# Second attention: values stationary in four 32-column array tiles, sums by a constant pattern, inverses spread by block transposes

## What is computed

```python
def _L1_xattn_ref(queries, keys, values, Wq, Wk, Wv, Wo):   # queries = layernorm(x), keys = values = ctx
    # 32 query heads of 16 columns, 8 key/value heads, 4 query heads share one
    q = (queries @ Wq).reshape(b, s, KV_HEADS, GROUP, HEAD_DIM)
    k = (keys @ Wk).reshape(b, s, KV_HEADS, HEAD_DIM)
    v = (values @ Wv).reshape(b, s, KV_HEADS, HEAD_DIM)
    scores = jnp.einsum('bqhgd,bkhd->bhgqk', q, k) * scale
    attn = jax.nn.softmax(scores, axis=-1)
    out = jnp.einsum('bhgqk,bkhd->bqhgd', attn, v)
    return out.reshape(b, s, EMBED) @ Wo

x = x + _L0_xattn_ref(_layernorm(x), ctx, ctx, ...)
x = x + _L0_ffn_ref(_layernorm(x), ...)         # 8 experts, the best 2 of each row
x = x + _L1_xattn_ref(_layernorm(x), ctx, ctx, ...)
x = x + _L1_ffn_ref(_layernorm(x), ...)         # gated, 1376 wide
```

## Time and profile before

| | |
|---|---|
| median of 3 runs | 975.94 us (974.81 to 982.37) |
| the profiled execution | 983.04 us, span from first to last instruction 981.3 us, mean TensorE clock 0.955 |
| busy PE, PEld | 916.7 us (93%), 759.9 us (77%) |
| busy DVE, ACT, POOL | 435.3 us (44%), 348.1 us (35%), 293.8 us (30%) |
| `attend` (L1450), matmuls | 512 instructions, 66.7 us busy |
| loads and stores of x and its normalized form in this stage | 256 KB each, 2.7 to 3.8 us to landing |

### The profile page before, as it was taken

One profiled execution on the slowest core, in us unless ns is written; L12 is line 12 of the kernel. 1 busy time (PEld: TensorE's weight loads), 2 busy tenths in 40 slices (PEclk: granted clock), 3 DMA queues, 4 the chain that ended last, 5 costly groups with the idle time before them and its releaser, 6 DMA issues. The chain is left out here.

```text
span 981.3 us, 16773 instructions
## 1 busy us (share of the span) xinstructions
PE 916.7 (93%) x6065; PEld 759.9 (77%) x6065; DVE 435.3 (44%) x866; ACT 348.1 (35%) x567; POOL 293.8 (30%) x415
## 2 busy tenths in 40 slices
PE   6999987899998799999999956999999999999997
PEld 4888876788887688888878845888788788878885
DVE  3988865344444556765657621222312122223112
ACT  3556643233332355555546522222111112111111
POOL 4588863000003665565654220111202000202000
PEclk9999998899998879999989976999999999999999
DMA  8566655794544232434422214111003001202001
GB/s 267 172 226 235 198 188 192 267 312 164 161 149 151 66 105 88 149 104 132 134 80 83 83 54 150 43 43 41 1 11 108 12 0 42 66 1 86 1 1 43
DMA packets 56801, 108.20 MB, mean 110 GB/s; under 512 B 8242, under 2 KB 12338, under 8 KB 56594
## 3 DMA queue, kind: packets, MB, share of 16 engines
q1 hardware_dynamic: 49954, 88.13, 27.8%
q0 software_dynamic: 5120, 16.78, 5.2%
q10 hardware_dynamic: 1648, 2.23, 0.6%
HBM read 67.99 MB, written 39.12 MB: 109 GB/s over the span
## 5 line engine op out<-in xcount | busy, mean ns | idle before, releaser
L1900 DVE SCALAR_TENSOR_TENSOR d_hid<-d_pup,d_b_up,d_silu 128x512 f32<-128x512 f32 (+1 forms) x44 | 33.0, 751 | 235.4 <-PE d_pup L1829 235.4
L1790 ACT ACTIVATE d_silu<-d_pgate,d_b_gate 128x512 f32<-128x512 f32 (+1 forms) x44 | 30.3, 689 | 154.7 <-PE d_pgate L1829 154.7
L1761 POOL TENSOR_TENSOR d_x_res<-d_x_res,d_b_down 128x512 f32<-128x512 f32 x16 | 22.0, 1405 | 187.1 <-DMA d_x_res<-x_after_attention 187.1
L1168 POOL DMA_INDIRECT c_y_in<-expert_results,y_at x32 | 32.7, 1023 | 145.6 <-POOLq L98 137.5
L1827 PE MATMUL d_pgate<-d_nT_hi,gate_up_hi 128*128 128x512 f32 (+1 forms) x176 | 71.5, 406 | 1.4 <-DVE d_nT_lo L1889 1.4
L1797 ACT ACTIVATE d_hid_hi<-d_hid 128x512 fp32r<-128x512 f32 (+1 forms) x44 | 27.8, 632 | 125.3 <-DVE d_hid L1900 125.3
L1829 PE MATMUL d_pgate<-d_nT_hi,gate_up_lo 128*128 128x512 f32 (+1 forms) x176 | 70.3, 400 | 0.0
L1828 PE MATMUL d_pgate<-d_nT_lo,gate_up_hi 128*128 128x512 f32 (+1 forms) x176 | 70.0, 397 | 0.0
L1859 PE MATMUL d_pdown<-d_down_hi,d_hid_hi 128*128 128x512 f32 (+1 forms) x176 | 69.5, 395 | 0.0
L1827 PE MATMUL d_pup<-d_nT_hi,gate_up_hi 128*128 128x512 f32 (+1 forms) x176 | 69.5, 395 | 0.0
L1829 PE MATMUL d_pup<-d_nT_hi,gate_up_lo 128*128 128x512 f32 (+1 forms) x176 | 69.3, 394 | 0.0
(11 more groups left out here) (271 smaller groups left out, 2145.8 us busy)
## 6 DMA issues: line engine op xcount, KB each, us to landing
b_rows<-expert_rows SPq DMA_DIRECT2D x39, 256.0 KB, 2.8
expert_results<-b_result SPq DMA_DIRECT2D x39, 256.0 KB, 2.5
a_wstage<-L_ffn_W_e SPq DMA_DIRECT2D x16, 512.0 KB, 4.2
c_stage<-gate_up SPq DMA_DIRECT2D x16, 344.0 KB, 3.2
late_x<-x_after_attention SPq DMA_DIRECT2D x16, 256.0 KB, 3.8
x_after_attention<-late_x SPq DMA_DIRECT2D x16, 256.0 KB, 3.4
norm_after_attention<-c_n_out SPq DMA_DIRECT2D x16, 256.0 KB, 3.3
d_n_in<-norm_after_attention SPq DMA_DIRECT2D x16, 256.0 KB, 2.8
```

What stands on the lines that cost most here:

```text
L1900: dve.scalar_tensor_tensor(hid[0:w, s % 2, :], pup[s % 2][0:w, :], b_up[0:w, i:i + 1], silu[0:w, s % 2, :], ALU.add, ALU.mult).then_inc(hi ...
```

## The change

- **`attend`**: the values are stationary, 32 columns of them (two heads of 16, block-diagonal over the two sequences' halves), and the turned probabilities are moving, 128 columns. The four j go to four array tiles of 128 rows by 32 columns, whose results lie in partitions 32j to 32j + 31. A second set of four products has a constant pattern own_rows stationary, which gives each sum 16 times. So there are eight products where there were four, and the result comes out already turned.
- **`transpose_attn` is gone**, with bank b2's part in it; the column of ones beside the values is gone, so KV_COLS falls from 400 to 384 (stored, loaded and cleared rows too).
- **DVE**: per b, `turn_sums` transposes 32x32 blocks of the sums from PSUM into turned (128x256), `invert_sums` inverts 16 columns, `spread_inverse` transposes them back, repeated 16 times each, into inverse (128x256), and `keep_attn` multiplies into attnT. Between `invert_sums` and `keep_attn` now stand `sum_x3` and `average_x3`, or `sum_x2` and `average_x2`.
- **ACT and DVE** read attnT (SBUF) for the high and the low part in place of bank b2.
- **Waits**: `transpose_probs(t, 1, 0)` waits for `q_rows_kept` of the next tile in place of `alo_kept`; `keep_attn` also waits for `ahi_kept`.

```diff
@@ -111,7 +111,7 @@
...
-KV_EARLY, KV_LATE, KV_COLS, X_RING = 8, 8, P + 16 * (HD + 1), 6
+KV_EARLY, KV_LATE, KV_COLS, X_RING = 8, 8, P + 16 * HD, 6
...
@@ -450,14 +450,14 @@
...
-                    act.wait_ge(kv_cleared, 6)
+                    act.wait_ge(kv_cleared, 2)
...
-                        ins = act.activation(values[64 * r:64 * r + 64, b, :, r, 0:HD], made[:, :, r, :], ACT.Copy)
+                        ins = act.activation(values[64 * r:64 * r + 64, b, :, r, :], made[:, :, r, :], ACT.Copy)
...
@@ -785,9 +785,6 @@
                 if i == 0:
                     dve.wait_ge(s_made, TILES)
                 dve.memset(blocks, 0.0).then_inc(kv_cleared, 1)
-                dve.wait_ge(kv_cleared, 3 * i + 1)
-                for r in range(2):
-                    dve.memset(blocks.rearrange("p (n r d) -> p n r d", r=2, d=HD + 1)[64 * r:64 * r + 64, :, r, HD:HD + 1], 1.0).then_inc(kv_cleared, 1)
 
             for m in range(-3, TILES + 3):
                 g = group_ending(m - 3)
@@ -1031,12 +1028,14 @@
...
-        q_rows, qT, attn, n_out = (sb(n, [P, DIM]) for n in ("q_rows", "qT", "attn", "n_out"))
+        q_rows, qT, attnT, n_out = (sb(n, [P, DIM]) for n in ("q_rows", "qT", "attnT", "n_out"))
+        turned, inverse = sb("turned", [P, 2, 256]), sb("inverse", [P, 256])
+        own_rows, own_zeroed = sb("own_rows", [P, 2 * HD]), sem("own_zeroed")
...
-        smax, rsum = sb("smax", [P, 2, 16]), sb("rsum", [P, 2, 2, KVH, 1])
+        smax, rsum = sb("smax", [P, 2, 16]), sb("rsum", [P, 2, 16, 1])
...
@@ -1287,10 +1286,9 @@
                 act.activation(probT[:, g, :], probs_bank(b, g)[:, :], ACT.Copy).then_inc(pt_kept, 1)
 
             def keep_high_attn(t):
-                act.wait_ge(at_made, t + 1)
+                act.wait_ge(o_kept, 2 * t + 2)
                 want(act, w_made, t)
-                act.activation(aT_hi[:, :].rearrange("p (g b q) -> p b g q", g=GROUP, b=2),
-                               b2[:, :].rearrange("p (b g q) -> p b g q", b=2, g=GROUP), ACT.Copy).then_inc(ahi_kept, 1)
+                act.activation(aT_hi[:, :], attnT[:, :], ACT.Copy).then_inc(ahi_kept, 1)
 
             def high_part(t):
                 act.wait_ge(gu_loaded[t % 2], full(t))
@@ -1416,9 +1414,10 @@
                 pe.wait_ge(exp_done, 2 * t + b + 1)
                 if b:
                     if g == 0:
-                        want(pe, alo_kept, t)
-                        if t == 0:
-                            pe.wait_ge(q_rows_kept, 2)
+                        if t + 1 < TILES:
+                            pe.wait_ge(q_rows_kept, t + 2)
+                        else:
+                            pe.wait_ge(pt_kept, 4 * t - 1)
                     elif t + 1 < TILES:
                         pe.wait_ge(q_kept, t + 2)
                 elif g:
@@ -1446,20 +1445,12 @@
                 pe.wait_ge(pt_kept, n + 1)
                 want(pe, o_kept, 2 * t + b)
                 for j in range(4):
-                    at = 136 * g + 34 * j
-                    mm = pe.matmul(po[:, at:at + 34], probT[:, g, P * j:P * j + P],
-                                   kv[:, t % EARLY, P + 136 * b + 34 * j:P + 136 * b + 34 * j + 34], start=True, stop=True)
+                    pe.matmul(po[32 * j:32 * j + 32, P * g:P * g + P], values_of(t)[:, b, j, :, :].rearrange("p r d -> p (r d)"),
+                              probT[:, g, P * j:P * j + P], start=True, stop=True)
+                for j in range(4):
+                    mm = pe.matmul(po[32 * j:32 * j + 32, 256 + P * g:256 + P * g + P], own_rows[:, :],
+                                   probT[:, g, P * j:P * j + P], start=True, stop=True)
                 mm.then_inc(o_made, 1)
-
-            def transpose_attn(t):
-                pe.wait_ge(o_kept, 2 * t + 2)
-                if t + 2 < TILES:
-                    pe.wait_ge(q_rows_kept, t + 3)
-                else:
-                    pe.wait_ge(pt_kept, 4 * t + 3)
-                for i in range(4):
-                    mm = pe.transpose(b2[:, P * i:P * i + P], attn[:, P * i:P * i + P], ident[:, :])
-                mm.then_inc(at_made, 1)
 
             def project(t):
                 if t == 0:
@@ -1493,8 +1484,6 @@
                     scores(m, 1)
                     transpose_probs(m, 0, 0)
                     transpose_probs(m, 0, 1)
-                if 0 <= m - 1 < TILES:
-                    transpose_attn(m - 1)
                 if m < TILES:
                     attend(m, 0, 0)
                 if m + 1 < TILES:
@@ -1552,25 +1541,32 @@
                 peak = smax[:, b, :].rearrange("p (r g x) -> p r g x", r=4, x=1).to_broadcast([P, 4, 4, 64])
                 dve.tensor_tensor(score[:, b, :].rearrange("p (r g e) -> p r g e", r=4, e=64), all_scores(), peak, ALU.subtract).then_inc(s_shifted, 1)
 
-            def heads():
-                return po[:, 0:272].rearrange("p (c h d) -> p c h d", c=2, h=KVH)
+            def turn_sums(t, b):
+                dve.wait_ge(o_made, 4 * t + 2 * b + 2)
+                dve.transpose(turned[:, b, :], po[:, 256:512]).then_inc(sums_turned, 1)
 
             def invert_sums(t, b):
-                dve.wait_ge(o_made, 4 * t + 2 * b + 2)
-                dve.reciprocal(rsum[:, b, :, :, :], heads()[:, :, :, HD:HD + 1]).then_inc(sum_step, 1)
+                dve.wait_ge(sums_turned, 2 * t + b + 1)
+                dve.reciprocal(rsum[:, b, :, :], turned[:, b, :].rearrange("p (n d) -> p n d", d=HD)[:, :, 0:1]).then_inc(sum_step, 1)
+
+            def spread_inverse(t, b):
+                n = 2 * t + b
+                dve.wait_ge(sum_step, n + 1)
+                want(dve, o_kept, n)
+                dve.transpose(inverse[:, :], rsum[:, b, :, :].to_broadcast([P, 16, HD])).then_inc(inverse_ready, 1)
 
             def keep_attn(t, b):
-                dve.wait_ge(sum_step, 2 * t + b + 1)
-                want(dve, at_made, t)
-                dve.tensor_tensor(attn[:, 256 * b:256 * b + 256].rearrange("p (c h d) -> p c h d", c=2, h=KVH), heads()[:, :, :, 0:HD],
-                                  rsum[:, b, :, :, :].to_broadcast([P, 2, KVH, HD]), ALU.mult).then_inc(o_kept, 1)
+                dve.wait_ge(inverse_ready, 2 * t + b + 1)
+                want(dve, ahi_kept, t)
+                want(dve, alo_kept, t)
+                dve.tensor_tensor(attnT[:, :].rearrange("p (g b q) -> p b g q", g=GROUP, b=2)[:, b, :, :],
+                                  po[:, 0:256].rearrange("p (g q) -> p g q", g=GROUP),
+                                  inverse[:, :].rearrange("p (g q) -> p g q", g=GROUP), ALU.mult).then_inc(o_kept, 1)
 
             def keep_low_attn(t):
                 dve.wait_ge(ahi_kept, t + 1)
                 want(dve, w_made, t)
-                order = "p (g b q) -> p b g q"
-                dve.tensor_tensor(aT_lo[:, :].rearrange(order, g=GROUP, b=2), b2[:, :].rearrange("p (b g q) -> p b g q", b=2, g=GROUP),
-                                  aT_hi[:, :].bitcast(F32).rearrange(order, g=GROUP, b=2), ALU.subtract).then_inc(alo_kept, 1)
+                dve.tensor_tensor(aT_lo[:, :], attnT[:, :], aT_hi[:, :].bitcast(F32), ALU.subtract).then_inc(alo_kept, 1)
 
             def add_attn(t):
                 dve.wait_ge(w_made, t + 1)
@@ -1586,9 +1582,10 @@
                 dve.bn_aggr(mv3[:, t % 2, :], stats3[:, t % 2, :]).then_inc(mv3_ready, 1)
 
             dve.memset(kv[:, :, P:KV_COLS], 0.0).then_inc(values_zeroed, 1)
-            dve.wait_ge(values_zeroed, 1)
+            dve.memset(own_rows[:, :], 0.0).then_inc(own_zeroed, 1)
+            dve.wait_ge(own_zeroed, 1)
             for r in range(2):
-                dve.memset(kv[64 * r:64 * r + 64, :, P:KV_COLS].rearrange("p s (n r d) -> p s n r d", r=2, d=HD + 1)[:, :, :, r, HD:HD + 1], 1.0).then_inc(values_zeroed, 1)
+                dve.memset(own_rows[64 * r:64 * r + 64, HD * r:HD * r + HD], 1.0).then_inc(values_zeroed, 1)
             keep_values(0)
             keep_values(1)
             low_weights(0)
@@ -1617,11 +1614,16 @@
                     sum_x2(2)
                     average_x2(2)
                 if 0 <= m - 1 < TILES:
+                    turn_sums(m - 1, 1)
                     invert_sums(m - 1, 1)
-                    keep_attn(m - 1, 1)
                 if 0 <= m - 2 < TILES:
                     sum_x3(m - 2)
+                if 0 <= m - 1 < TILES:
+                    spread_inverse(m - 1, 1)
+                if 0 <= m - 2 < TILES:
                     average_x3(m - 2)
+                if 0 <= m - 1 < TILES:
+                    keep_attn(m - 1, 1)
                 if m < TILES:
                     max_scores(m, 1)
                     shift_scores(m, 1)
@@ -1630,11 +1632,16 @@
                 if 0 <= m - 1 < TILES:
                     keep_low_attn(m - 1)
                 if m < TILES:
+                    turn_sums(m, 0)
                     invert_sums(m, 0)
-                    keep_attn(m, 0)
                 if m + 3 < TILES:
                     sum_x2(m + 3)
```

(5 more changed lines are left out.)

6 lines of the change are left out of this document (3 added, 3 removed).

## The result

The changed kernel takes 974.3 us (median of 20 runs, 969.63 to 979.12) against 979.38 us for the kernel before, measured beside it (median of 20, 974.45 to 988.4): ratio 0.9945, 95% interval 0.9925 to 0.9966. That is 5.4 us less, half a per cent, within the 1% called "no change" above. Predicted were 3.7 us less and 972.2 us. When both were measured again later, the medians were 971.46 and 980.3 us, the ratio 0.993 (0.9905 to 0.9954). The profiled execution of the changed kernel spans 975.7 us, against 981.3.

The account below looks back on a forecast made before the run. A ring of store, load, additions, gathers and low part bounds the middle, TensorE the other tiles. Savings of 1.2 us before the ring, 2.3 by its end and 1.4 behind give 3.7 off 975.94: 972.2 us, range 966 to 984.

Parts of the forecast that it names:

- What bounds the kernel: Second attention: TensorE bounds only the first four or five and last four or so tiles, at 13.85 us each.
- The ring of store, load, additions, gathers and low part: Middle of second attention: x3 store, x1 load and GpSimd work wait on each other, nine rounds of 15.1 us.
- `attend` at 0.66 us: TensorE, attention products: 16 instructions over four column tiles take as long as `scores`; tile saves 0.5 us.
- the lower one: Lower bound for `attend` on TensorE: full overlap of four column tiles, 0.44 us; the upper bound was 1.78.
- The wait for ScalarE in place of the transposes: TensorE before `attend(m, 0, 0)`: 0.4 us waiting for ScalarE's first `keep_probT` replaces 0.44 us of removed transposing.
- VectorE: Block transposes at 0.42 us add 1.7 us a tile, hidden except once at the ring's end and at the stage's end.
- a wait of `attend` for `keep_attn`: Sign against the forecast: reciprocals or `keep_attn` on VectorE appear as releaser of TensorE's `attend`.
- The end chain: End of second attention, reciprocal to projection, uncovered: 3.2 us instead of 2.21, costing 1.0 us once.
- The ring's term: Middle of second attention: the ring repeats its nine rounds; 2.3 us earlier by its end, 1.2 from before it.
- No overlap: Rival, TensorE: column tiles do not overlap, tile 17.85 us, TensorE bounds everywhere, 1031 us; chance 0.15.
- Full overlap: Rival, TensorE: column tiles overlap fully, saving 1.4 us a tile, 966.5 us; chance 0.13.
- Clock: Rival: longer TensorE waits in ring-bound tiles lower its clock, excess 0.6 us over nine tiles, 978 us; chance 0.15.

Follow-up runs that it names:

- e1: Changed kernel with SyncE's store of x3 moved ahead of the load of the next gate_up part: 953.5 us, ratio 0.9763 to the kernel before.
- e2: Kernel before with SyncE's store of x3 moved ahead of the load of the next gate_up part: 970.02 us, ratio 0.9915 to the unedited kernel before.
- e3: Changed kernel with all small attention products written to one column tile instead of four (results partly wrong): 1031.93 us, ratio 1.0544 to the kernel before.
- e10: Changed kernel with the small attention products on two column tiles instead of four (half the heads wrong): 982.48 us, ratio 1.0027 to the kernel before.
- e9: Changed kernel measured and profiled once more, unchanged: 971.46 us, ratio 0.993 to the kernel before.
- e4: Changed kernel with values and sums products issued back to back for each column tile, not all values first: 972.77 us, ratio 0.995 to the kernel before.

## Why the prediction was right, and where its terms were off

**What bounds the kernel: right, and shown.** The ring of store, load, additions, gathers and low part sets the middle. Its nine rounds kept their 15 us while TensorE's tile fell by 1 us, and one move in SyncE's queue released them (e1, e2).

**`attend` at 0.66 us: mis-sized, it is 0.46.** The step that failed is the choice of `scores` as nearest row because it was "the only row with four tiles at once", and the use of its whole length as the price of each `attend`. `scores` takes 0.66 us for 16 instructions here too, but that is a block with its exit, and a single `attend` with its exit takes 0.58 (373.28 to 373.86). Row tiles are not slower in themselves. The trace's single starts go in groups of four in both, at 371.28, 371.50, 371.61 and 371.72 in `scores` and at 373.28, 373.41, 373.52 and 373.63 in `attend`: 0.11 us a group, but for the first step of `scores`, 0.21. The better bound for what is repeated was the lower one: the instruction's 0.11 us divided by four. e3 and e10 show that this division holds. The entry was sized rightly, 0.1 us: the four products ahead of the pair take 0.59 us instead of 0.49. What was left out is an exit of each block, 0.11 us (368.28 less 367.95 and 0.22). Paired and single blocks with their exits are 1.01 + 0.58 + 0.58 = 2.17 us, the two entries outside the wait 0.2.

The rule weighed in the prediction fails here. The Trainium skill, "TensorE: Matmul & The Clock Gate", The mechanism, lets a weight load overlap running products only where the row group differs. Four column tiles share one, and the trace has 29 ns for each instruction, loads included.

**The wait for ScalarE in place of the transposes: right.** From the start of `transpose_probs` to `attend(m, 0, 0)` are 1.34 us (371.94 to 373.28), where the transposes of probabilities took 0.93: 0.41 us, predicted 0.4. The saving is 3.85 - 2.17 - 0.2 - 0.41 = 1.07 by these rows, and 0.98 from tile to tile. Predicted were 0.5.

**VectorE: right in size, nearly right in cover.** Block transposes take 0.445 and 0.426 us, taken at 0.42. In the middle they are hidden. `add_attn` comes 1.4 us behind the start of `sum_x2` (0.8 before; 0.84 more were predicted, it is 0.6), as the queue of VectorE shows:

```profile
463.23 0.25 DVE L1550 RECIPROCAL c_rsum<-c_turned 128x16 f32<-128x16 f32 x1
465.73 0.69 DVE L1508 BATCH_NORM_STATS2 c_stats<-late_x 128x6 f32<-128x512 f32 x1 [2.24 <-POOL late_x L1178]
466.34 0.43 DVE L1556 STREAM_TRANSPOSE c_inverse<-c_rsum 128x256 f32<-128x256 f32 x1
466.69 0.14 DVE L1513 BATCH_NORM_AGGREGATE c_mv<-c_stats 128x2 f32<-128x6 f32 x1
466.80 0.42 DVE L1562 TENSOR_TENSOR c_attnT<-c_po,c_inverse 128x256 f32<-128x256 f32 x1
467.14 0.68 DVE L1573 TENSOR_TENSOR late_x<-c_bank,late_x 128x512 f32<-128x512 f32 x1
```

Spread and product stand behind the wait for x2. The prediction looked for a wait of `attend` for `keep_attn` as a sign against it. There is one, ahead of the first `add_attn`: 0.61 us in this profile, 2.02 in e9. It was not costed. The end chain, turned sums to projection, is 2.90 us now (567.24 to 570.14), against 2.21: 0.7 more, predicted 1.0.

```profile
567.24 0.45 DVE L1546 STREAM_TRANSPOSE c_turned<-c_po 128x256 f32<-128x256 f32 x1 [1.59 <-PE c_po L1451]
```

```profile
570.14 0.76 PE L1374 MATMUL c_bank<-c_proj_hi,c_aT_hi 128*128 128x512 f32 x1 [2.96 <-ACT c_aT_hi L1291]
```

**The sum.** The prediction had 1.2 us up to the first load in the ring, 2.3 by the end of the ring and 3.7 in all. In the traces, counted from the start of the stage, the first of POOL's waiting additions comes 3.4 us earlier (79.2 to 75.8 us), the last of them 3.9 (214.9 to 211.0), and the last `add_attn` 8.5. With its second profile the kernel before has 4.9 in place of that 8.5; against the second profile of the changed kernel the two give 15.4 and 11.7. So these profiles do not size the stage's total. Two of its terms can be read, and both were too small. The saving of a warm tile was half the true one. And the lead, with `attend` of the first two tiles in it, was counted as two warm tiles and 0.2 us for "a pair at the lower clock", 1.2 together. It fell by about 3 (57.6 and 57.7 to 54.5), of which the change of clock between executions is part and can't be divided off: e9 has 51.3, and e2, which changes nothing in the lead of the kernel before, 56.0. The ring's term, nothing gained in nine rounds, was right to 0.5 us, and it is the large one: without it the medians of the two kernels differ by 16.5 us (e1, e2).

The forecast of 972.2 us lies 2.1 below the first median and 0.7 above the second, 971.46. That it came so near is in part luck: the three runs of before shown ahead of it had a median of 975.94, and twenty had 979.38. The saving, 3.7 us forecast, was 5.4 and by the second ratio 6.9.

**The rivals.** On TensorE the rival with a chance of 0.13 came true and not the forecast's own step; the ring kept most of the difference out of the time. No overlap: it was priced at 1031 us, and e3, which forces it, took 1031.93. Full overlap: it happened on TensorE, and its price, 966.5 us from 975.94, a saving of 9.4, was too high against the 5.4 and 6.9 measured; it too left out the exits, 0.33 us of its 1.4 a tile. Clock: four tiles ran at 0.88 or 0.89 after waits of 1.9 to 2.8 us. The three of them at 0.89 cost nothing, since PE is busy for 14.1 us in them and the ring needs 15. At the end of the stage the clock did cost: the last two parts took 22.6 us at 0.86 and 0.69, and 20.5 at 1.00 and 0.83 in e9.

## What to carry to other kernels

Ask of each saved microsecond whether the engine it is saved on is what the next wait waits for: here nine tiles of sixteen gave nothing back until a store was moved ahead of a load in a queue, and that move, which computes nothing, was worth two to three times the change (1.8% by e1 against the 0.55% and 0.7% of its two measurements). Where small products share a moving side but not an output, put them in different column tiles: two halve and four quarter the time, and their order does not matter. To invert values that repeat over columns, bring them together first if that costs less than the inversion: here 0.87 us for two transposes against the 1.5 us that 240 more columns cost.

## What the runs showed of the hardware

- Products of 32 stationary columns in four column tiles ran at 29 ns an instruction, on two at 56, on one at 111 (0.46, 0.89 and 1.77 us for 16). Four in a row on one tile did not hold up the next tile's, which started ahead of them (e4). Four row tiles of 32 rows (`scores`) went at the same 0.11 us for four.
- A change between blocks of full shape and column tiles cost about 0.1 us at the entry and 0.11 at the exit.
- A reciprocal of 128x256 from PSUM took 1.76 us, of 128x16 0.25; a block transpose of 128x256 0.43 to 0.45.
- Of eight waits of TensorE in one profile, those up to 1.05 us left the products behind them at full speed (four in 0.63 us), and those of 1.91 to 2.76 us did not (0.89 to 1.08). In another execution of the same kernel waits of 1.83, 1.99 and 2.18 us were followed by 0.63. So a wait near 2 us decides nothing by itself.
- With the same instructions, the last part of the stage took 8.26, 9.81 and 10.67 us at mean clocks of 1.00, 0.83 and 0.70, and the lead 51.3 or 54.5. A single profile can't judge a change of 3 us that lies there.
